# Adding the sixteen state products in pairs on VectorE before TensorE sums them, in a Mamba and mixture-of-experts layer

## The reference

```
xn = layernorm(x)
xz = xn @ in_proj^T; x, z = split(xz)             # 1024 channels each
x  = silu(conv4(x)); z = silu(conv4(z))           # depthwise, 4 taps
dt, B, C = split(x @ x_proj^T)                    # 64, 16 and 16 wide
delta = softplus(dt @ dt_proj^T + bias)
h[d,n] = exp(delta[d] * A[d,n]) * h[d,n] + delta[d] * x[d] * B[n]   # for each token, n = 0..15
y[d]   = sum over n of h[d,n] * C[n]  +  D[d] * x[d]
s  = concat(y, z) @ out_proj^T
g  = silu( top-2 of 8 experts (gelu, hidden width 512) + a shared expert )   # all on xn
out = x + s * g
```

## Time and profile before

| | us |
|---|---|
| median of 3 runs | 4488.08 (4483.39 to 4489.57) |
| the profiled execution | 4480.74 |
| its span on the slowest core, core 4 | 4479.1 |
| spans of the other cores | 4450.7 to 4468.5 |
| PE busy (matmuls) | 2568.1, 57% |
| DVE busy | 2273.5, 51% |
| ACT busy | 2025.3, 45% |
| POOL busy | 261.0, 6% |
| mean granted clock of PE, eight cores | 0.767 to 0.781 |

### The profile page before, as it was taken

The page is one execution under the profiler, slowest core; times in us unless marked ns, Lnnn a source line. Parts: engine busy times, 40 slices in busy tenths (PEclk is TensorE's granted clock), DMA queues, the critical chain, the costliest instruction groups (busy, mean ns, idle before and its releaser), DMA issues.

```text
span 4479.1 us, 70523 instructions; the slowest of 8 cores (4450.7 to 4479.1 us)
## 1 busy us (share of the span) xinstructions
PE 2568.1 (57%) x17792; PEld 1922.8 (43%) x17792; DVE 2273.5 (51%) x2949; ACT 2025.3 (45%) x4233; POOL 261.0 (6%) x386
## 2 busy tenths in 40 slices
PE   1204656575665656566565766656575665656564
PEld 1103544353444535345443544445353444435443
DVE  0204364563836456383644638364563836456384
ACT  1304363544636354463645446363544636354462
POOL 0100010100001010100101010010101001010100
PEclk9557878787787878778787867877787887878788
DMA  7796433343433334344333434333333443334342
GB/s 109 109 110 156 124 122 116 118 137 110 131 125 121 123 123 133 110 131 135 120 123 118 128 115 131 127 118 119 128 128 112 133 131 118 122 122 127 120 133 92
DMA packets 329924, 549.76 MB, mean 123 GB/s; under 512 B 20457, under 2 KB 170090, under 8 KB 324530
## 3 DMA queue, kind: packets, MB, share of 16 engines
q1 hardware_dynamic: 319554, 473.49, 33.7%
q0 software_dynamic: 9968, 71.77, 8.5%
HBM read 557.31 MB, written 46.47 MB: 135 GB/s over the span
## 4 chain that ended last, share of the span: by engine, by line
PE 31%; ACT 23%; DMA 18%; issue 14%; DVE 6%; another core or an unknown queue 6%; POOL 2%; SPq 0%; DVEq 0%; ACTq 0%; POOLq 0%
PE P L259 30%; ACT dA L817 9%; DMA sb_in<-blob_in 6%; DMA sb_w<-blob_w 5%; ACT scrb L933 3%; DMA sb_out<-blob_out 3%; ACT L933 2%; DMA x_f<-x_t 2%; ACT xzh L580 2%; POOL delta L697 2%; PE P L526 1%; DMA bc_dram<-bcB 1%; DMA sb_cd<-blob_cd 1%; DVE h_b L846 1%
## 5 line engine op out<-in xcount | busy, mean ns | idle before, releaser
L846 DVE TENSOR_TENSOR_SCAN h_b<-dA,carry,dBx 128x1024 bf16<-128x1024 f32 x480 | 1128.3, 2351 | 82.8 <-DVE dA L842 82.4
L817 ACT ACTIVATE dA<-delta,A_neg 128x256 f32<-128x256 f32 x2048 | 858.6, 496 | 615.5 <-DVE fixt L829 584.9
L259 PE MATMUL P<-xn_b,sb_w 128*128 128x256 bf16 x4096 | 655.7, 331 | 562.1 <-ACT scrb L933 423.7
L259 PEld LDWEIGHTS P<-xn_b,sb_w 128*128 128x128 bf16 x4096 | 466.8, 117 | 748.6 <-issue 623.6
L259 PE MATMUL P<-scrb,sb_w 128*128 128x256 bf16 x4096 | 482.5, 276 | 52.7 <-DMA sb_w<-blob_w 52.2
L259 PEld LDWEIGHTS P<-scrb,sb_w 128*128 128x128 bf16 x4096 | 401.9, 99 | 115.9 <-issue 65.1
L810 DVE TENSOR_TENSOR dBx<-u_b,Bb 128x4096 bf16<-128x4096 bf16 x128 | 293.9, 2296 | 251.2 <-DMA Bb<-bc_dram 196.1
L259 PE MATMUL P<-xzh,sb_cd 128*128 128x256 bf16 x1024 | 205.4, 378 | 324.7 <-ACT xzh L580 147.4
L933 ACT ACTIVATE scrb<-P,b1c 128x256 bf16<-128x256 f32 x512 | 242.4, 473 | 306.2 <-PE P L259 269.3
L259 PE MATMUL P<-xn_b,sb_in 128*128 128x256 bf16 (+1 forms) x2176 | 286.0, 288 | 159.2 <-DMA sb_in<-blob_in 158.4
L943 DVE TENSOR_TENSOR scrb<-scrb,ge_all 128x1024 bf16<-128x1024 bf16 x128 | 88.5, 691 | 537.6 <-ACT scrb L933 277.1
(11 more groups left out here) (115 smaller groups left out, 2441.8 us busy)
## 6 DMA issues: line engine op xcount, KB each, us to landing
sb_w<-blob_w SPq DMA_DIRECT2D x512, 512.0 KB, 4.3
sb_in<-blob_in SPq DMA_DIRECT2D x256, 256.0 KB, 3.3
sb_out<-blob_out SPq DMA_DIRECT2D x128, 512.0 KB, 4.8
sb_cd<-blob_cd SPq DMA_DIRECT2D x128, 256.0 KB, 3.7
Bb<-bc_dram POOLq DMA_DIRECT2D x16, 1024.0 KB, 5.0
Cb<-bc_dram POOLq DMA_DIRECT2D x16, 1024.0 KB, 6.9
blob_w<-w_w POOLq DMA_DIRECT2D x2, 8192.0 KB, 123.3
out<-stage SPq DMA_DIRECT2D x32, 512.0 KB, 3.2
```

Source lines behind the costliest of these rows:

```text
L259: return eng.matmul(out_ap, lhsT, rhs, start=first, stop=last, skip_group_check=True)
L817: return eng.activation(sb["dA"][:, slot * 256:(slot + 1) * 256], sb["delta"][:, g * 256:(g + 1) * 256], AF.Exp, scale=sb["A_neg"][:, g * ...
L846: return eng.tensor_tensor_scan(sb["h_b"][:, q0 * 256:(q0 + 4) * 256], apv(sb["dA"], s0 * 256, [[1, 1024]]), apv(sb["dBx"], dko + q0 * 256 ...
```

## The change

After hc, DVE gets one more instruction for each group. It adds the odd states of the 16 products to the even ones, in place in dBx, and rounds to bf16. The identity matmuls then run over the eight even states only. So per group one DVE operation with 8 x 256 = 2048 outputs on each partition is added and 8 of 16 identity matmuls are removed. There are 16 x 8 = 128 groups in all.

```diff
             S.add("dve", fhc, reads=("h", "Cb", dk), writes=(dk,), tag="hc%d.%d" % (i, g))
+            def fps(eng, dko=dko):
+                ev = apv(sb["dBx"], dko, [[512, 8], [1, 256]])
+                od = apv(sb["dBx"], dko + 256, [[512, 8], [1, 256]])
+                return eng.tensor_tensor(ev, ev, od, ALU.add)
+            S.add("dve", fps, reads=(dk,), writes=(dk,), tag="hp%d.%d" % (i, g))
 
         def idents_phase(i, g, first=False):
             dpar = g % 2
             dko = dpar * 4096
             dk = "dBx:p%d" % dpar
             half = dpar * 256
-            for n in range(DSTATE):
+            for n in range(0, DSTATE, 2):
                 mm(ps["P7"][:, half:half + 256], sb["ident_b"][:, :],
```

## The result

| | before | after |
|---|---|---|
| median, us | 4486.95 (8 runs, 4480.98 to 4513.98) | 4596.66 (8 runs, 4592.43 to 4604.05) |
| ratio | | **1.0246**, 95% interval 1.0234 to 1.0258 |
| span of the profiled execution | 4479.1 | 4597.9 |
| spans of the eight cores, mean | 4462.4 | 4582.5 |
| mean granted clock of PE, eight cores | 0.767 to 0.781 | 0.751 to 0.763 |

The account below looks back on a forecast made before the run. DVE's scan bounds the expert loop, PE alone the stretch from the last scanning step. 64.3 - 13.9 + 19.5 + 20.1 - 0.4 = 89.6 us on the profiled 4480.7 gives a median of 4578 us; range 4545 to 4606.

Parts of the forecast that it names:

- What bounds: Expert loop: DVE's scan, then ACT, then PE; from the last scanning step, 17.01 us of nothing but PE.
- 1.34 us per exposed pair-add: On DVE, each uncovered pair-add costs 1.34 us: 1.22 us of work plus its wait for the product before it.
- Groups 0 and 1: Before the first gate product: 1.3 us a chunk after 1.15 us of slack, in 15 chunks +19.5 us.
- Group 5: Last scanning step: pair-add hidden by 0.37 us before PE's identity matmuls; eight fewer of these save 13.9 us in all.
- Group 7: Before the next chunk's gate, top-2, DRAM bounce and POOL softplus: 1.34 us in full, 15 times, +20.1 us.
- Group 6's pair-add: Before a scan that waits 21.60 us for the exponentials: free.
- Groups 2 to 4 and PE's saving: Expert loop: three uncovered pair-adds, 4.02 us a chunk (+64.3 us), less 0.87 us for PE's eight removed matmuls (-13.9 us).
- Rival (b): DVE's 26.8 us idle before dbx are real waits for PE's matmuls, which pair-adds would fill: 4551 us; chance 0.09.
- (a): PE's clock stays low longer in w1 before group 5, up to 2 us in 16 chunks: 4605 us; chance 0.10.
- (c): The pair-add runs on DVE at the f32 rate, 2.29 + 0.11 us each: 4691 us; chance 0.06.
- (d): PE's work decides every step, so 111 us go and DVE's additions hide: 4377 us; chance 0.04.
- (e): The add is too short to see or moved off the path: no difference, 4488 us; chance 0.03.

Follow-up runs that it names:

- The merged pair: The kernel before and the changed kernel, each with one wait for each semaphore on every instruction: 4423.77 us (ratio 0.9863) and 4530.85 us (1.0096).

## Why the prediction was right, point by point

**What bounds.** DVE's scan in the expert loop, PE in the stretch behind it, as read. Shown by the pair: adding DVE work alone gives a ratio of 1.0286, sparing PE work alone 0.9954.

**1.34 us per exposed pair-add.** Right: 1225 ns, and 1.30 to 1.37 us a step where no waits interfere.

**Where they land.** Groups 0 and 1: +1.39 for 1.3. Group 5: hidden, as said; its pair-add ends 0.99 us (mean) before PE comes to the identity matmuls, where 0.37 was read. Group 7: +1.62 for 1.34, and all but 0.21 of it went away when the pair-add was moved behind the gate, so the path through gate, bounce and POOL was right. Group 6's pair-add stayed where it was in that run and stands in the same stretch, so it costs 0.21 at most, near enough to the nothing that was said. The 0.28 above the 1.34 isn't explained.

**Groups 2 to 4 and PE's saving**, 4.02 - 0.87 = 3.15 us, measured 4.40: this is the mis-sized term. The step that was too small is "hc, pair-add, L943, dbx, scans. Nothing covers them": I priced the new instruction and its wait for hc, but not the waits queued behind it. They had been hidden under hc, and the wait moved them out. Three holes of 1.08 or 1.43 us opened, less those of 0.5 to 0.9 us before dbx that closed. The four steps grew by 7.33 us, where four pair-adds make 5.36; with merged waits they grew by 5.34. That settles the 1.97 us between. PE's part gave 2.93 us back, where the forecast has the hidden pair-add and the matmuls, 2.21; so 1.25 us were left.

PE's own 0.87 us came to 0.57 in the changed kernel (32.44 to 31.87 us from the identities of group 5 to the projection). The missing 0.30 is the late gate product: w2's first matmul now starts 0.41 us after the one before it, in place of 0.11. The merged pair is a warning all the same. There is no train there, and yet its loop is 4.16 us longer and not 3.15, since PE's part gave back 1.19 only. The loop's term would have been a microsecond too small there too, for a reason in PE's stretch that stays open.

**Rival (b)** was half true: the 26.8 us of holes before dbx did vanish (1.0 left). But they were no waits for PE, the pair-adds didn't fill them (with all 16 matmuls kept they stand), and more opened elsewhere. **(a)**: the 30 matmuls of w1 before group 5 took 5.15 us for 5.08 from the first of them to the identities, in the mean of chunks 1 to 15 and all cores; in single chunks it's 4.3 to 6.0 us in both kernels. The granted clock was 0.63 there, 0.64 before, so the clock was not it. **(c)**, **(d)** and **(e)** are refuted by the 1225 ns of the pair-add, by PE's longer waits and by the 2.5%.

The forecast of 4578 was 19 us short of 4597. Of the 1.67 us missing per chunk (7.46 less 5.79) some 1.25 stand in the loop, 0.28 before the gate, and the rest is small. That the time came out inside the range owes something to PE's part: without the 0.72 us that it gave back beyond the forecast, 1.97 us of train a chunk would have come to some 4608 (an estimate, 4597 and 15 x 0.72), just outside.

## What to carry to other kernels

Ahead of an instruction on DVE stood its waits, and they took the sequencer's time even when their values had been reached long ago. That cost next to nothing as long as DVE had something to execute, and it showed as soon as an instruction that must wait for its predecessor was put in between. So when a dependent instruction is added, count the waits behind it, not only its duration, and keep one wait for each semaphore (here 1.4% for one line). And moving work from an engine that waits (PE) to the one that is waited for (DVE) can pay only where the added work is hidden; even there, for group 5 alone, the gain of 5 to 9 us in the traces was too small for the times.

## What the runs showed of the hardware that was not expected

- A wait for a value long reached costs DVE's sequencer 0.07 us: 2.31 us for 33, 4.52 for 66, 1.21 for 17. The waits are in the trace, 0.069 us apart, and one place in every 128 instructions of DVE's stream added 0.35 us where it fell into such a train (29 times on each core).
- The trace names the semaphore's owner as releaser of such a hole (PE, 1.08 us), though nothing was waited for. Its size recurs, 1.08 or 1.43 to 1.45 us, whatever PE is doing; that is the sign, and the semaphore instructions listed by their source line are the proof.
- An in-place sum of two interleaved halves (runs of 256 bf16, step 512) took 1225 ns for 2048 elements, on the line between the products of 1024 (0.69 us) and 4096 elements (2.29 us).
- The 9330 waits spared on SP changed the time by 0.05%, inside the interval.
